# One masking pass of VectorE over four heads instead of two passes over two heads each, in the attention stage of a graph kernel

## The reference, cut to what matters

```python
q = (embeds[rows] @ qW).reshape(e, HEADS, dh)        # HEADS = 4, dh = 24
k = (embeds[cols] @ kW).reshape(e, HEADS, dh)
v = (embeds[cols] @ vW).reshape(e, HEADS, dh)
scores = jnp.clip(jnp.einsum('ehd,ehd->eh', q, k), -10.0, 10.0)
exp_s = jnp.exp(scores)
norms = jax.ops.segment_sum(exp_s, rows, num_segments=nvar)[rows]
w = exp_s / (norms + 1e-08)
res = jax.ops.segment_sum(w[:, :, None] * v, rows, num_segments=nvar).reshape(nvar, d)
return embeds + res
```

## Time and profile before

| what | value |
|---|---|
| median of 3 runs | 5337.36 us (5336.82 to 5350.37) |
| the profiled execution, its own time | 5337.36 us |
| its span, first to last instruction | 5335.6 us |
| busy shares of the span | PE 80%, DVE 67%, POOL 54%, ACT 49% |
| first and last start of the changed instruction (line 2276) | 3892.8 and 5326.5 us |
| instructions of that line | 1204, two for each of 602 steps |

### The profile page before, as it was taken

The page is one execution under the profiler, slowest core; times in us unless marked ns, Lnnn a source line. Parts: engine busy times, 40 slices in busy tenths (PEclk is TensorE's granted clock), DMA queues, the critical chain, the costliest instruction groups (busy, mean ns, idle before and its releaser), DMA issues.

```text
span 5335.6 us, 96545 instructions
## 1 busy us (share of the span) xinstructions
PE 4277.4 (80%) x35389; PEld 2642.7 (50%) x35389; DVE 3576.6 (67%) x6066; ACT 2612.3 (49%) x4219; POOL 2870.6 (54%) x2968
## 2 busy tenths in 40 slices
PE   4777799999998666666666666665599999999999
PEld 2777789989897333333333333333533333333334
DVE  6899943344435555555555555554699999999999
ACT  4766610010101333333333333332389999999998
POOL 3100000000002777777777777776278888888887
PEclk9999999999999787878777777777799999999999
DMA  3233379869896444444444444443012222122221
GB/s 72 121 147 153 144 280 359 330 261 340 311 370 202 135 131 136 131 136 130 136 129 137 129 137 129 137 129 105 21 56 58 58 58 59 58 58 58 58 58 39
DMA packets 296274, 760.02 MB, mean 142 GB/s; under 512 B 81000, under 2 KB 183464, under 8 KB 289704
## 3 DMA queue, kind: packets, MB, share of 16 engines
q1 hardware_dynamic: 217352, 595.36, 31.5%
q0 software_dynamic: 78624, 160.79, 11.2%
HBM read 589.77 MB, written 166.22 MB: 142 GB/s over the span
## 4 chain that ended last, share of the span: by engine, by line
DVE 31%; POOL 29%; PE 14%; issue 14%; DMA 9%; DVEq 1%; ACT 1%; SPq 0%; POOLq 0%; ACTq 0%
POOL GA L747 28%; DVE VA L2276 22%; PE p_e L1118 8%; DMA GA<-adj 4%; DMA VA<-adj 4%; PE p_e L1250 1%; PE p_mm L1035 1%; PE p_tr L1265 1%; POOL VA L747 1%; DVE R L1787 1%; DVE M L1789 1%; DVE GA L1789 1%; DVE VA L1787 1%; DVE R L1789 1%; DVE GA L1787 1%
## 5 line engine op out<-in xcount | busy, mean ns | idle before, releaser
L747 POOL DMA_INDIRECT GA<-table_mg,VA x1568 | 1491.9, 951 | 1543.2 <-DMA table_mg<-VA 1040.5
L2276 DVE TENSOR_TENSOR VA<-VA,p_mm 128x1024 f32<-128x1024 f32 (+1 forms) x1204 | 1385.0, 1212 | 30.7 <-POOL VA L845 7.1
L845 POOL TENSOR_SCALAR VA<-VA 128x1024 f32<-128x1024 f32 (+1 forms) x1204 | 1242.0, 1040 | 288.8 <-ACT VA L1552 218.4
L1156 PE MATMUL p_e<-GA,C 128*128 128x384 f32 x896 | 561.5, 802 | 692.5 <-DMA GA<-table_mg,VA 692.5
L1156 PEld LDWEIGHTS p_e<-GA,C 128*128 128x128 f32 x896 | 272.2, 319 | 956.6 <-DMA GA<-table_mg,VA 760.8
L1552 ACT ACTIVATE VA<-p_e,score_unit 128x1024 f32<-128x1024 f32 x602 | 669.9, 1113 | 98.6 <-PE p_e L1250 98.1
L2076 DVE TENSOR_TENSOR M<-GA,p_mm 128x1344 f32<-128x1344 f32 x112 | 174.1, 1555 | 765.9 <-ACT GA L1500 765.8
L1265 PE MATMUL p_tr<-VA,GA 128*32 128x512 f32 (+1 forms) x5096 | 641.1, 580 | 3.5 <-ACT GA L1564 3.1
L2102 DVE SCALAR_TENSOR_TENSOR R<-R,keep,M 128x97 f32<-128x97 f32 x1568 | 513.6, 328 | 125.5 <-issue 10.7
L1500 ACT ACT_TABLE_LOAD x112 | 143.7, 1283 | 921.5 <-PE p_e L1156 921.5
L1250 PE MATMUL p_e<-T,GA 32*128 32x512 f16 x4632 | 487.4, 379 | 3.9 <-DVE VA L2263 1.4
(11 more groups left out here) (267 smaller groups left out, 7049.9 us busy)
## 6 DMA issues: line engine op xcount, KB each, us to landing
GA<-adj SPq DMA_DIRECT2D x98, 800.0 KB, 6.1
VA<-adj SPq DMA_DIRECT2D x98, 800.0 KB, 6.1
run_m<-R SPq DMA_DIRECT2D x112, 700.0 KB, 3.9
GA<-adj SPq DMA_DIRECT2D x98, 768.0 KB, 6.1
VA<-adj SPq DMA_DIRECT2D x98, 768.0 KB, 6.1
H<-adj SPq DMA_DIRECT2D x56, 896.0 KB, 5.2
adj<-GA SPq DMA_DIRECT2D x25, 1568.0 KB, 5.2
adj<-VA SPq DMA_DIRECT2D x24, 1568.0 KB, 5.1
```

Source lines behind the costliest of these rows:

```text
L747: pool.indirect_dma_start(out=to, out_offset=None, in_=of, in_offset=bass.IndirectOffsetOnAxis(ap=at, axis=0)).then_inc(s, 16)
L845: pool.tensor_scalar(e, e, HIGH, LOW, ALU.min, ALU.max).then_inc(clipped, 1)
L1156: pe.matmul(p_h[k][0:CH, 0:4 * D].rearrange("p (a f) -> p a f", a=2), C[0:CH, C_ID:C_ID + CH], G[0:CH, h, 2 * k:2 * k + 2, 0:2 * D], start ...
L2276: dve.tensor_tensor(e, e, p_mm[n % 2][:, 0:cols_of(n)].unsqueeze(1).to_broadcast([P, 2, cols_of(n)]), ALU.mult).then_inc(weighed, 1)
```

## The change

DVE masks all four heads of a step in one instruction. It waits until both clips of the step are done, counts one in `weighed`, and PE's two waits for `weighed` count steps instead of halves. No other instruction changes, nor any tile.

```diff
 def mask(n):
-                    wait(pe, weighed, 2 * (n - 1))
+                    wait(pe, weighed, n - 1)
...
 def values(n):
-                            if i == 0 and e % 2 == 0:
-                                pe.wait_ge(weighed, 2 * n + e // 2 + 1)
+                            if i == 0 and e == 0:
+                                pe.wait_ge(weighed, n + 1)
...
 def attention():                     # DVE
                 for n, (b, ds) in enumerate(STEPS_A):
                     dve.wait_ge(mask_ready, n + 1)
-                    for pair in (0, 1):
-                        e = slot[n % SLOTS][:, 2 * pair:2 * pair + 2, 0:cols_of(n)]
-                        dve.wait_ge(clipped, 2 * n + pair + 1)
-                        dve.tensor_tensor(e, e, p_mm[n % 2][:, 0:cols_of(n)].unsqueeze(1).to_broadcast(
-                            [P, 2, cols_of(n)]), ALU.mult).then_inc(weighed, 1)
+                    e = slot[n % SLOTS][:, :, 0:cols_of(n)]
+                    dve.wait_ge(clipped, 2 * n + 2)
+                    dve.tensor_tensor(e, e, p_mm[n % 2][:, 0:cols_of(n)].unsqueeze(1).to_broadcast(
+                        [P, HEADS, cols_of(n)]), ALU.mult).then_inc(weighed, 1)
```

## The result

The changed kernel took 5380.85 us (median of 4, 5372.93 to 5384.10) against 5343.86 us for the kernel before in the same session (median of 4, 5336.82 to 5352.88). The ratio is 1.0063, 95% interval 1.0046 to 1.0081. The forecast was 5353.7 us, 0.31% slower than 5337.36, with a range of 5346 to 5379. So the direction was right and the cost, 37.0 us for 16.3, over twice the forecast. The measured time itself lies 2 us above the range. The kernel before also measured 6.5 us more than the 5337.36 from which the range was counted; the ratio, taken from 5337.36, gives 5371 us, inside it.

A forecast was written before the change was run, and what follows sets the result against it. A PE-ACT loop of 4.70 us for two steps was taken as the bound. Group ends 12.7, start 1.0, end 0.6 and scatter 2 us summed to 16.3 over 5337.36: 5353.7 us, range 5346 to 5379.

The forecast's parts named there:

- What bounds the kernel: Ordinary attention steps: PE and ACT alone set 2.35 us a step; DVE and POOL follow with some room.
- The loop of PE and ACT: ACT's pair and head 2, then PE's head 2, values, mask and scores: 4.70 us for two steps, without DVE.
- The duration of the new pass: DVE's one masking instruction over four heads, 2048 elements: 2.28 us, from the line through measured durations.
- The dead heat: Ordinary steps: three-step loop through DVE's merged pass takes 7.04 us against PE and ACT's 7.05; steps stay 2.35 us.
- The 2 us put down for scatter: Ordinary steps, with no room left between the loops: 0.003 us a step over 588 steps, 2 us.
- The ends of groups: Where a group is finished, DVE's pass ends 1.06 us later and delays PE's head 3: twelve times, 12.7 us.
- everything behind is later by as much: After a group's last pass, line 2263, head 3, its exponential and the values each come 1.06 us later.
- Start and end: First pass of the stage ends 1.0 us later, the last 0.5, plus 0.1 for matmuls no longer running ahead.
- The new loop: Rival: the three-step loop through the merged pass takes 7.19 us, 28 us more, 5379 us; chance 0.15.
- The forecast's own case: Whole kernel: 5353.7 us, 0.31% slower, with bounds of 5349 to 5360 us; chance 0.65.
- DVE as the bound: Rival: DVE sets the step, so merging saves 0.07 us in each of 602 steps, 39 us, 5298 us; chance 0.07.
- the hidden case: Rival: something else holds head 3 at group ends, so only 1.6 us is lost, 5339 us; chance 0.13.

The follow-up runs named there:

- the single clip: Changed kernel with POOL's two clips a step also made one over four heads: one execution, 5846.17 us, stage 166 us over the changed kernel.
- the short head 2: ACT's exponentials left out for half of head 2's columns, one execution each: kernel before 5598.72 us, changed kernel 5634.23 us, against 5631.12 us for the uncut kernel before.
- the filled wait: Changed kernel with four unread 512-column matmuls in PE's wait for head 3 at the twelve group ends: 5659.55 us, ratio 1.0041 to the kernel before.

## Why the prediction was right, and where it fell short

- *What bounds the kernel.* Right. The loop of PE and ACT, 4.70 us for two steps, held when DVE's work was nearly halved, and gave back 0.21 of 0.216 us when ACT's part of it was cut.
- *The duration of the new pass.* 2.28 us forecast, 2288 ns measured.
- *The dead heat.* Right: 2.35 us a step, evenly spaced, masks waiting for DVE. The 2 us put down for scatter came to 1.2, and as single late starts of DVE, which the room had covered before.
- *The ends of groups.* The mechanism and the wait were right (1.08 us each against 1.06), the term was mis-sized: 12.7 us forecast, some 26 measured (the distance of groups is (5219.7 - 4027.8)/10 - 116.85 = 2.34 us longer; twelve times this is 28, and 1.2 of it are the late starts). The step that failed is the sentence "everything behind is later by as much". What is behind was also slower: at the lower clock values took 1.60 us and not 1.06. The prediction noted the clock of 1.00 and did not ask what an idle time of 1.4 us would do to it, though the trace of before shows PE at the lower level where it had waited at the start of the stage: its four mask matmuls took 0.61 us there, at a clock of 0.50, and 0.40 in the earlier trace rows.
- *Start and end.* 1.6 us forecast, 3.4 measured: 1.1 at the end for 0.6, and 2.3 at the start for 1.0, where the later mask cost 1.1, about as forecast, and the lower clock, again left out, 1.2 more.
- *The rivals.* The new loop did not decide. It is real, as the single clip and the short head 2 show, but at 7.05 us it only draws level. That the measured time lies near that rival's 5379 is a coincidence of sums, and so it is luck that the range held the result: its upper end was priced by a loop that did not decide. The forecast's own case, 5349 to 5360 us, did not hold it. DVE as the bound, and the hidden case, are both refuted.

Of the 31 us in the profile, some 13 are the clock behind the waits of the group ends (the filled wait gives them back), some 13 the waits, 2.3 the start, 1.2 the late starts of DVE and 1.1 the end. None of the versions that do the whole work beats the kernel before: halves up to the end of each group bring the merged pass level with it, which fits, as DVE's work is not in the loop that sets the step.

## What to carry to other kernels

An engine at 98% whose instructions start right after their inputs are ready can be a follower, as DVE is here; add up the loop that gives the measured period before taking work from it. Merging two instructions saves a fixed cost on the engine but delays the first half's result by a whole producer instruction: find who waits for that, and whether the lateness is carried on to a place without room. Where a wait of TensorE grows, look whether the granted clock falls behind it; filling the wait with matmuls whose result nobody reads tells this apart.

## What the runs showed of the hardware

In these kernels TensorE's clock fell behind idle times of 1.4 us at ten of twelve ends of groups in the changed kernel (the two stretches above show either case; what decides is open), and stayed at 1.00 after 0.91 us and after 0.40 us idle with four matmuls behind. The Trainium skill (TensorE: Matmul & The Clock Gate, on the second failure mode) tells of a kernel in which short idle times between groups of matmuls, coming often, make the clock go back and forth between its levels. The trace agrees in that a short idle time can be followed by a fall; here one came only every 118 us or so.

An instruction of DVE that reads two operands from SBUF was held up by POOL. Line 2268 (X <- X + VA, 384 columns) takes 0.60 us in the kernel before, 12 times, and in the changed one:

```profile
L2268 DVE TENSOR_TENSOR X<-X,VA 128x384 f32<-128x384 f32 x12 | 14.0, 1168 | 1.1
```

```profile
4503.51 1.04 POOL L845 TENSOR_SCALAR VA<-VA 128x1024 f32<-128x1024 f32 x1 [0.65 <-ACT VA L1552]
...
4503.73 1.22 DVE L2268 TENSOR_TENSOR X<-X,VA 128x384 f32<-128x384 f32 x1
```

POOL's clip began at 4503.51 and ended at 4504.55, and DVE's addition, begun at 4503.73, ended at 4504.95, 0.40 us after it. Before, it began at 4483.55 near a clip's end (4481.54 + 2.19 = 4483.73) and ended 0.42 us behind that. The masked pass, which reads one operand from PSUM, shows nothing of this beside the same clips. The Trainium skill (SBUF — State Buffer, Who interferes with whom, and its summary) says that of a DVE instruction with two SBUF inputs and a GpSimd instruction that reads SBUF the second to be issued is blocked until the first finishes; by that rule, the trace agrees. It costs nothing here, as it lies behind line 2263.
